# Attention readout and a top-2 expert layer: four experts' numbers to a register word

## Chip, cores and metric

The kernel runs on one core of a Trainium2 chip. The metric is the time of one execution on the device in microseconds, lower is better. A measurement is several runs of the same program, and its median stands for it.

## What is computed

`x` is 64 x 128 rows of 512 numbers in float32. Two steps follow each other, each added to its input:

```python
x = x + _L0_xattn_ref(_layernorm(x), ctx_2048, mask)     # 64 batches of 128 rows, 128 context rows each
x = x + _L0_ffn_ref(_layernorm(x), G, gate_w, up_w, down_w, lora_A, lora_B)

# the second step, with 8 experts of width 64, top 2, and a low-rank part of 16
scores = softmax(einsum('bsh,he->bse', x, G))
value, indices = top_k(scores, 2)
w = einsum('bsk,bske->bse', value, one_hot(indices, 8))
gated = silu(einsum('bsh,efh->bsef', x, gate_w)) * einsum('bsh,efh->bsef', x, up_w)
out = einsum('bsef,bse,ehf->bsh', gated, w, down_w)
lr  = einsum('bsh,erh->bser', x, lora_A)
out = out + einsum('bser,bse,ehr->bsh', lr, w, lora_B)
```

## The kernel before

**The sweep** (`for t in range(SWEEP)` on each engine, up to about 220 us) goes over the 64 batches of 128 tokens: layer norm, attention, the new x, and the router's logits. It picks each token's two experts and scatters the token's row (x, weights, row numbers) to a table in HBM, `x1_rows`, sorted by expert. The first expert of a token (the lower number) belongs to the first pass, the second to the second pass.

**The block loop** (`for t in range(TICKS)`) then works on blocks of 128 rows of one expert each: NQ = 70 blocks in a pass, 140 in all, and 143 ticks. SyncE loads block q's rows into one of RI = 21 slots (`load_block`), TensorE, ScalarE and VectorE work on it over four ticks, and GpSimd scatters the result: in the first pass 516 KB of rows to `z_rows`, in the second 256 KB to the output. In tick t TensorE does, in this order: `turn_h(t)`, four transposes (L478); `gate_up(t-1)`, four float32 matmuls of 144 columns that the hardware does in eight pieces (L494), whose weights lie at an address that depends on the block's expert; the register load `expert_at(t+1)` (L487); `turn_gated(t-2)`, one transpose (L501); `down(t-3)`, two matmuls of 512 columns (L510, L511), again at the expert's address. ScalarE copies the transposed rows (L658), does the tanh (L664), the rounded half of the gated values (L670) and, in the first pass, the layer norm (L651). VectorE makes `t` (L1061), `gg` (L1066), the other half `ggT_b` (L1073) and two copies (L1077, L1078), and adds the block's result to its rows (L1088), with one more instruction, L1087, where a block may overlap the next. `down` waits for L1078 of the tick before (semaphore `again`), L501 for L1066 of the tick before (`gg_ready`).

Which expert a block belongs to is known only once the tokens have been counted. VectorE works out a table with a column for each of the two passes: the expert times WE = 576 (the width of an expert's weights) and the first row. It stands with blocks along the partitions. `turn_table` on TensorE turns it by four matmuls against the identity, and `keep_table` on VectorE copies partition 64 of the result to `table_i`, where registers are loaded from. This happens twice: for the first KA = 38 blocks of each pass during the sweep (t = 54), and for the other 32 in tick 27 of the block loop; VectorE's arithmetic for the second table is spread over ticks 8 to 23. TensorE loads a block's expert by `pe.value_load` (L487), SyncE its first row (L286): each a register load, one fused register instruction and an assertion that the value is in range. Nothing schedules the work: the order of each engine is the order written here.

## Time and profile before

| what | us |
|---|---|
| median of 3 runs (545.64 to 547.66) | 546.95 |
| the profiled execution, device time | 547.48 |
| its span from first to last instruction | 545.7 |
| TensorE matmuls busy | 513.9 |
| VectorE busy | 477.7 |
| ScalarE busy | 357.8 |
| GpSimd busy | 287.0 |

All times inside an execution are read against its span, which is 1.8 us shorter than its device time. The sweep ends at about 220 us. The first pass of the block loop takes TensorE from there to about 390 us and the second pass to about 540. "PEld" is the row of TensorE's weight loads, of which each matmul has one, and a q behind an engine (PEldq, SPq) its sequencer, which executes register loads, register arithmetic and waits itself.

### The profile page before, as it was taken

Reading aid. Unit: us, or ns where it says so; the run is one execution under the profiler, and the core shown is the slowest. Engines: PE = TensorE matmul, PEld = TensorE weight load, DVE = VectorE, ACT = ScalarE, POOL = GpSimd, SP = SyncE. Lnnn points to the kernel's source line nnn. Section 1 sums busy time; section 2 is a strip of 40 time slices with the busy share of each in tenths; the row PEclk is TensorE's granted clock in tenths of the full one; section 3 lists DMA queues with packets and bytes.
Section 4 is the critical chain, followed back from the end, with each engine's and each line's share of the span. In section 5 each row is a group of like instructions: output and inputs, shape, how many; then the busy total and the mean of one; then the engine's idle time right before and its main releaser. Section 6 shows DMA issues by size and latency. Waiting matters only on the chain.

```text
span 545.7 us, 16991 instructions
## 1 busy us (share of the span) xinstructions
PE 513.9 (94%) x4040; PEld 441.5 (81%) x4040; DVE 477.7 (88%) x1919; ACT 357.8 (66%) x991; POOL 287.0 (53%) x398
## 2 busy tenths in 40 slices
PE   8999999999999999698999899999999999999994
PEld 7788877778877877587788788888899999999883
DVE  5899999999999997668898888888899999999875
ACT  4778888888887876566677677777544444444441
POOL 4237677776776665644444344344444445444434
PEclk9999999999999999999999999999999999999988
DMA  8999999999999979999997999857999999999722
GB/s 312 355 323 360 387 389 361 401 386 393 388 392 384 320 246 299 397 376 400 360 328 278 365 364 330 301 215 261 411 413 416 416 415 417 415 416 412 290 97 77
DMA packets 65611, 189.13 MB, mean 347 GB/s; under 512 B 9582, under 2 KB 9710, under 8 KB 65520
## 3 DMA queue, kind: packets, MB, share of 16 engines
q1 hardware_dynamic: 44352, 120.20, 59.9%
q0 software_dynamic: 20800, 67.65, 31.6%
q8 instruction: 40, 0.66, 0.5%
q14 instruction: 51, 0.42, 0.2%
q10 hardware_dynamic: 368, 0.21, 0.1%
HBM read 114.03 MB, written 78.73 MB: 353 GB/s over the span
## 4 chain that ended last, share of the span: by engine, by line
PE 80%; issue 7%; DVE 5%; ACT 4%; another core or an unknown queue 1%; POOL 1%; DMA 0%; POOLq 0%; DVEq 0%; ACTq 0%
PE rd L494 12%; PE bank L494 12%; PE bank L478 11%; PE bank L348 8%; PE rd L510 8%; PE rd L511 6%; PE rd L393 6%; PE rd L394 4%; PE rd L501 4%; PE bank L329 4%; PE bank L361 3%; ACT xn L588 1%; PE bank L385 1%; ACT pT L559 1%; PE bank L346 1%
## 5 line engine op out<-in xcount | busy, mean ns | idle before, releaser
L658 ACT COPY hT<-bank 128x512 f32<-128x512 f32 x140 | 82.0, 586 | 61.8 <-PE bank L478 51.5
L494 PE MATMUL bank<-wg_sb,hT 128*128 x560 | 80.5, 287 | 1.9 <-ACT hT L658 1.8
L494 PE MATMUL rd<-wg_sb,hT 128*128 x560 | 82.2, 291 | 0.1
L1193 POOL DMA_INDIRECT x_rows<-xe x64 | 65.3, 1020 | 29.7 <-issue 21.4
L494 PEld LDWEIGHTS rd<-wg_sb,hT 128*128 128x128 f32 x560 | 74.4, 194 | 0.4 <-issue 0.3
L494 PEld LDWEIGHTS bank<-wg_sb,hT 128*128 128x128 f32 x560 | 72.6, 190 | 2.6 <-issue 2.6
L348 PE MATMUL bank<-cc_sb,xnT 128*128 128x136 f32 x512 | 73.0, 285 | 0.0
L510 PE MATMUL rd<-dn_a,ggT_a 128*128 x140 | 67.6, 483 | 1.6 <-DVE ggT_b L1078 1.2
L348 PEld LDWEIGHTS bank<-cc_sb,xnT 128*128 128x128 f32 x512 | 63.7, 190 | 2.1
L1208 POOL DMA_INDIRECT out_x<-z_shared x41 | 40.1, 977 | 43.4 <-issue 26.8
L1088 DVE SCALAR_TENSOR_TENSOR z_shared<-rd,z_shared 128x512 f32<-128x512 f32 x77 | 57.7, 749 | 1.9 <-PE rd L511 0.2
L1205 POOL DMA_INDIRECT z_rows<-z_own x34 | 32.9, 967 | 50.1 <-DVE z_own L1088 41.5
L1205 POOL DMA_INDIRECT z_rows<-z_shared x36 | 34.7, 965 | 46.5 <-DVE z_shared L1088 38.2
L511 PE MATMUL rd<-dn_b,ggT_b 128*128 x140 | 55.9, 399 | 0.0
L588 ACT ACTIVATE xn<-x_sb,norm 128x512 f32<-128x512 f32 x64 | 51.7, 808 | 1.1 <-POOL std L1145 1.1
L1088 DVE SCALAR_TENSOR_TENSOR z_own<-rd,z_own 128x512 f32<-128x512 f32 x63 | 47.2, 749 | 1.5
L501 PE MATMUL rd<-const_sb,gg 128*96 128x128 f32 x140 | 39.1, 279 | 9.8 <-issue 6.4
L751 DVE SCALAR_TENSOR_TENSOR xe<-rd,rinv,x_sb 128x512 f32<-128x512 f32 x64 | 47.7, 745 | 0.6 <-issue 0.6
L693 DVE BATCH_NORM_STATS2 st<-x_sb 128x6 f32<-128x512 f32 x64 | 43.7, 682 | 4.6 <-DMA x_sb<-in_x 4.3
L478 PEld LDWEIGHTS bank<-const_sb,z_shared 128*128 128x128 f32 x308 | 38.7, 142 | 10.7 <-issue 0.2
L478 PE MATMUL bank<-const_sb,z_shared 128*128 128x128 f32 x308 | 46.4, 273 | 0.0
L393 PE MATMUL rd<-cc_sb,pT 128*128 128x256 f32 x128 | 43.8, 424 | 1.2 <-ACT pT L559 0.6
(168 smaller groups left out, 1202.1 us busy)
## 6 DMA issues: line engine op xcount, KB each, us to landing
cc_sb<-in_cc SPq DMA_DIRECT2D x64, 532.0 KB
z_shared<-z_rows SPq DMA_DIRECT2D x41, 516.0 KB
x_sb<-in_x SPq DMA_DIRECT2D x64, 256.0 KB
z_own<-z_rows SPq DMA_DIRECT2D x29, 516.0 KB
z_shared<-x_rows SPq DMA_DIRECT2D x36, 260.0 KB
z_own<-x_rows SPq DMA_DIRECT2D x34, 260.0 KB
z_rows<-pad SPq DMA_DIRECT2D x8, 516.0 KB
wg_sb<-in_wg SPq DMA_DIRECT2D x8, 288.0 KB
```

The costliest lines, as they stand in the source:

```text
L348: mm = pe.matmul(sc_ps[:, 0:S + E], xnT[:, n % 2, k, :], by_feature(n, k, S + E), start=False, stop=(k == KD - 1))
L393: pe.matmul(rd_ps[n % 2][:, RD:512], pT[:, n % 2, :], cc_sb[:, n % RC, 0:512 - RD], start=True, stop=True)
L478: mm = pe.transpose(hT_ps[q % 2][:, k * P:(k + 1) * P], rows_of(q)[:, k * P:(k + 1) * P], ident)
L494: mm = pe.matmul(gu_ps[q % 2][:, 0:GU], hT[:, q % 2, k, :], wg_flat[:, bass.ds(at + k * GU, GU)], start=(k == 0), stop=(k == KD - 1))
L501: pe.transpose(gT_ps[0:KG, 0:P], gg[:, q % 2, :], ident).then_inc(ggT_done, 1)
L510: pe.matmul(y_ps[j][:], ggT_a[:, j, :], a_flat[:, bass.ds(at, D)], start=True, stop=False)
L511: pe.matmul(y_ps[j][:], ggT_b[:, j, :], b_flat[:, bass.ds(at, D)], start=False, stop=True).then_inc(y_done, 1)
L588: act.activation(xn[:, n % 2, :], x_sb[:, n % RX, :], ACT.Identity, scale=norm[:, m % 2, 0, b, 1:2], bias=norm[:, m % 2, 0, b, 0:1]).then_ ...
L658: act.copy(hT[:, q % 2, :, :], hT_ps[q % 2][:].rearrange("p (k s) -> p k s", k=KD)).then_inc(hT_ready, 1)
L1088: dve.scalar_tensor_tensor(out=row[:, D:2 * D], in0=y_ps[q % 2][:], scalar=row[:, weight:weight + 1], in1=row[:, D:2 * D], op0=ALU.mult, o ...
L1193: pool.indirect_dma_start(out=x1_rows[:, :], out_offset=rows_at(row, ROW1), in_=row, in_offset=None, bounds_check=ROWS - 1, oob_is_err=Fal ...
L1205: pool.indirect_dma_start(out=z_rows[:, :], out_offset=rows_at(row, D + ROW2), in_=row, in_offset=None, bounds_check=ROWS - 1, oob_is_err= ...
```

## The change

The word that TensorE loads no longer holds one expert times 576 but the experts of up to four consecutive blocks, three bits each. A pass has 38 and 32 blocks in its two tables, thus 10 and 8 groups, and both passes 36 groups. `turn_table` makes the words: for the two expert columns it multiplies by a constant matrix, `PACK`, that holds 1, 8, 64 and 512 for a group's four blocks, where the identity stood. VectorE's `keep_table` copies words and first rows apart, to `packed` and `first_row`. `expert_at` loads a word at the first block of a group (blocks 0, 4, 8 ... 36, 38, 42 ... 66 of a pass), keeps it in a register, and takes the expert out by a division, a remainder and a multiplication by 576. The constants grow by 18 columns. SyncE's loads of first rows are as they were, from the other tile.

```diff
@@ -59,6 +59,11 @@
+GB, EB = 4, 3
+assert E <= 1 << EB
+GROUPS = [range(at, min(at + GB, hi)) for lo, hi in ((0, KA), (KA, NQ)) for at in range(lo, hi, GB)]
+EARLY_GROUPS = -(-KA // GB)
...
@@ -137,7 +142,8 @@
-        expert, table, table_i = sb("expert", [2]), sb("table", [4]), sb("table_i", [4, NQ], I32)
+        expert, table, first_row = sb("expert", [2]), sb("table", [4]), sb("first_row", [2, NQ], I32)
+        packed = sb("packed", [2, len(GROUPS)], I32)
...
-                first = sp.value_load(table_i[KEPT:KEPT + 1, 2 + k, at:at + 1], min_val=0, max_val=ROWS - P)
+                first = sp.value_load(first_row[KEPT:KEPT + 1, k, at:at + 1], min_val=0, max_val=ROWS - P)
...
-            def turn_table(i, lo, hi):
+            def turn_table(i):
+                (lo, hi), (first, last) = blocks_of(i), groups_of(i)
                 pe.wait_ge(table_ready, 2 * i + 2)
                 for k in range(4):
-                    at = TABLES[i] + k * (hi - lo)
-                    mm = pe.matmul(rt_ps[:, at:at + hi - lo], table[:, k:k + 1].broadcast_to([P, P]), ident[:, lo:hi], start=False, stop=True, skip_group_check=True)
+                    what = const_sb[:, PACK + first:PACK + last] if k < 2 else ident[:, lo:hi]
+                    at = TABLES[i] + (k * (last - first) if k < 2 else 2 * (last - first) + (k - 2) * (hi - lo))
+                    mm = pe.matmul(rt_ps[:, at:at + what.shape[1]], table[:, k:k + 1].broadcast_to([P, P]), what, start=False, stop=True, skip_group_check=True)
                 mm.then_inc(tabT_done, 1)
...
+            word = {}
             def expert_at(q):
                 k, at = divmod(q, NQ)
+                g = next(i for i, group in enumerate(GROUPS) if at in group)
                 if q == 0:
                     pe.wait_ge(tabT_ready, 1)
                 if q == KA:
                     pe.wait_ge(tabT_ready, 2)
-                return pe.value_load(table_i[KEPT:KEPT + 1, k, at:at + 1], min_val=0, max_val=(E - 1) * WE)
+                if at == GROUPS[g].start:
+                    word[0] = pe.value_load(packed[KEPT:KEPT + 1, k, g:g + 1], min_val=0, max_val=(1 << EB * GB) - 1)
+                return pe.snap(word[0] // (1 << EB * (at - GROUPS[g].start)) % (1 << EB) * WE, min_val=0, max_val=(E - 1) * WE)
...
-                dve.tensor_scalar(table[:, 0:2], expert[:], float(WE), None, ALU.mult).then_inc(table_ready, 1)
+                dve.tensor_scalar(table[:, 0:2], expert[:], 1.0, None, ALU.mult).then_inc(table_ready, 1)
...
-            def keep_table(i, lo, hi):
+            def keep_table(i):
+                (lo, hi), (first, last) = blocks_of(i), groups_of(i)
+                at = TABLES[i] + 2 * (last - first)
                 dve.wait_ge(tabT_done, i + 1)
-                dve.tensor_copy(table_i[KEPT:KEPT + 1, :, lo:hi],
-                                rt_ps[KEPT:KEPT + 1, TABLES[i]:TABLES[i] + 4 * (hi - lo)].rearrange("p (k q) -> p k q", k=4)).then_inc(tabT_ready, 1)
+                dve.tensor_copy(packed[KEPT:KEPT + 1, :, first:last], rt_ps[KEPT:KEPT + 1, TABLES[i]:at].rearrange("p (k g) -> p k g", k=2))
+                dve.tensor_copy(first_row[KEPT:KEPT + 1, :, lo:hi],
+                                rt_ps[KEPT:KEPT + 1, at:at + 2 * (hi - lo)].rearrange("p (k q) -> p k q", k=2)).then_inc(tabT_ready, 1)
...
+    for i, group in enumerate(GROUPS):
+        consts[list(group), PACK + i] = 2.0 ** (EB * np.arange(len(group)))
```

TensorE's queue in tick 27, from the last pieces of `gate_up` over the register load, `turn_gated`, `down` and the second table to the next tick. Before:

```order
L494 ISA
L494 MATMUL bank2<-wg_sb,hT 128x144
L487 TENSOR_LOAD table_i
L487 ISA x2
L501 MATMUL rd0<-const_sb,gg 96x128
L510 REGISTER_ALU
L510 MATMUL rd1<-dn_a,ggT_a 128x512
L511 REGISTER_ALU
L511 MATMUL rd1<-dn_b,ggT_b 128x512
L434 MATMUL bank3<-const_sb,table 128x32 x4
L478 MATMUL bank0<-const_sb,z_own 128x128 x4
```

The same place in the change, block 28 beginning a word, where L515 is `gate_up`, L507 the load, L522 `turn_gated`, L531 and L532 `down`, L449 `turn_table` and L493 `turn_h`:

```order
L515 ISA
L515 MATMUL bank2<-wg_sb,hT 128x144
L507 TENSOR_LOAD packed
L507 ISA x2
L522 MATMUL rd0<-const_sb,gg 96x128
L531 REGISTER_ALU
L531 MATMUL rd1<-dn_a,ggT_a 128x512
L532 REGISTER_ALU
L532 MATMUL rd1<-dn_b,ggT_b 128x512
L449 MATMUL bank3<-const_sb,table 128x8 x2
L449 MATMUL bank3<-const_sb,table 128x32 x2
L493 MATMUL bank0<-const_sb,z_own 128x128 x4
```

And in the tick after it in the change, where block 29 takes its expert out of the word that is there:

```order
L515 ISA
L515 MATMUL rd0<-wg_sb,hT 128x144
L522 MATMUL rd0<-const_sb,gg 96x128
L531 REGISTER_ALU
L531 MATMUL rd1<-dn_a,ggT_a 128x512
L532 REGISTER_ALU
L532 MATMUL rd1<-dn_b,ggT_b 128x512
L493 MATMUL bank1<-const_sb,z_shared 128x128 x4
```

The load and its two ISA rows (the fused instruction and the assertion) are gone between `gate_up` and `turn_gated` in three ticks of four, and no row has come for taking the expert out: these operations are part of the ISA row ahead of a block's first matmul of `gate_up`. That row holds two register operations before, and four or five in the change.

VectorE's queue in the sweep where the first table is copied, before and then in the change (L815 is L794, L756 is L735):

```order
L794 MAX_INDEX which<-top,lg 128x8
L964 CAST table_i<-bank 1x4x38
L735 ISA masked,rowmin<-bank,zeros 128x128
L735 ISA rowmin 128x1
L742 RECIPROCAL rinv<-rowsum 128x1
```

```order
L815 MAX_INDEX which<-top,lg 128x8
L987 CAST packed<-bank 1x2x10
L988 CAST first_row<-bank 1x2x38
L756 ISA masked,rowmin<-bank,zeros 128x128
L756 ISA rowmin 128x1
```

One copy of 152 elements has become one of 20 and one of 76; in the block loop one of 128 becomes one of 16 and one of 64.

## Rows read from the trace of the kernel before

**Rows 1.** The page, part 1: engine, busy us (share of the span), instructions.

```profile
PE 513.9 (94%) x4040; PEld 441.5 (81%) x4040; DVE 477.7 (88%) x1919; ACT 357.8 (66%) x991; POOL 287.0 (53%) x398
```

**Rows 2.** By stretch: PE, PEld, DVE, ACT, POOL busy; clock, DMA share, GB/s.

```profile
235.00:312.00 77.00, 71.69 (x485) 60.64 (x483) 65.67 (x231) 52.84 (x127) 33.77 (x35) 1.00 0.95 350
312.00:401.00 89.00, 86.88 (x592) 75.06 (x591) 76.37 (x256) 62.56 (x150) 37.57 (x39) 1.00 0.88 321
401.00:509.00 108.00, 108.00 (x808) 100.07 (x807) 101.29 (x341) 51.50 (x162) 52.10 (x55) 1.00 1.03 415
...
150.00:187.00 37.00, 35.53 (x317) 29.43 (x316) 35.90 (x186) 29.71 (x87) 25.44 (x40) 1.00 1.01 375
```

**Rows 3.** Line L501 in 235:312, 312:401 and 401:509, with two idle rows (both TensorE rows together).

```profile
L501 PEld LDWEIGHTS rd<-const_sb,gg x31: 123/124/127, 236.0 to 310.4; 128*96 128x96 f32 x31
...
  issue: 11.9, 26
...
L501 PEld LDWEIGHTS rd<-const_sb,gg x40: 123/124/128, 312.7 to 400.9; 128*96 128x96 f32 x40
...
  issue: 6.2, 18
...
L501 PEld LDWEIGHTS rd<-const_sb,gg x54: 124/127/129, 400.9 to 507.4; 128*96 128x96 f32 x54
```

**Rows 4.** TensorE's weight loads by line, 235:312 and 312:401: busy, mean ns | idle before, releasers.

```profile
L510 PEld LDWEIGHTS rd<-dn_a,ggT_a 128*128 128x128 f32 x31 | 5.8, 187 | 3.1 <-issue 1.2
L501 PEld LDWEIGHTS rd<-const_sb,gg 128*96 128x96 f32 x31 | 3.9, 124 | 8.1 <-issue 7.6 <-DVE gg L1066 0.4
...
L510 PEld LDWEIGHTS rd<-dn_a,ggT_a 128*128 128x128 f32 x39 | 7.3, 187 | 3.4 <-issue 0.6
L501 PEld LDWEIGHTS rd<-const_sb,gg 128*96 128x96 f32 x40 | 5.0, 125 | 5.4 <-issue 4.6
```

**Rows 5.** Line L487 in the same stretches: ns min/median/max, first and last start.

```profile
L487 PEldq TENSOR_LOAD <-table_i x31: 297/766/1424, 236.9 to 311.7; - x31
...
L487 PEldq TENSOR_LOAD <-table_i x40: 298/616/1257, 311.7 to 400.0; - x40
L487 PEldq FUSED_REGOPS  x40: 151/151/151, 312.2 to 400.4; - x40
...
L487 PEldq TENSOR_LOAD <-table_i x54: 296/328/523, 401.9 to 508.3; - x54
```

**Rows 6.** Weight loads in order of time, 338.9 to 341.9, and its first register load.

```profile
339.02 1.04 PEld L494 LDWEIGHTS rd<-wg_sb,hT 128*128 128x128 f32 x8
340.31 0.12 PEld L501 LDWEIGHTS rd<-const_sb,gg 128*96 128x96 f32 x1 [0.24 <-issue]
340.52 0.19 PEld L510 LDWEIGHTS rd<-dn_a,ggT_a 128*128 128x128 f32 x1
...
341.42 0.67 PEld L494 LDWEIGHTS bank<-wg_sb,hT 128*128 128x128 f32 x5
...
L487 PEldq TENSOR_LOAD <-table_i x1: 842/842/842, 339.0 to 339.0; - x1
```

**Rows 7.** VectorE: largest waits in 235:401, and one copy of the tick of rows 6.

```profile
DVE t L1061 <- ACT th L664: 11.5, 31, 1.7
DVE t L1061 <- issue: 1.4, 2, 1.1
...
339.54 0.22 DVE L1078 CAST ggT_b<-ggT_a 32x128 fp32r<-32x128 f32 x1
```

**Rows 8.** Added work's nearest rows: L494's register operations (340.9:341.3), L964, L931, the constants.

```profile
L494 PEldq FUSED_REGOPS  x3: 42/46/46, 341.0 to 341.2; - x3
...
L964 DVE CAST table_i<-bank x2: 290/301/312, 187.7 to 292.7; 1x152 int32<-1x152 f32 x1, 1x128 int32<-1x128 f32 x1
...
L931 DVE TENSOR_SCALAR table<-expert x2: 163/181/199, 184.2 to 284.1; 128x2 f32<-128x2 f32 x2
...
const_sb<-in_consts ACTq DMA_DIRECT2D x1, 179.5 KB, 3.3
```

More of the change, by code:

```diff
@@ L81 @@
 RI = RO + RS
-IDENT, BEFORE, BASE, ROW0, LAST0, IOTA, NEXT, PART, SIGN, LOW, IDS, STRIPS = np.cumsum(
-    [0, P, P, 2 * E, 2 * E, 2 * E, E, SEG, 1, 1, 1, TB]).tolist()
-NCONST = STRIPS + 2 * E
+IDENT, BEFORE, BASE, ROW0, LAST0, IOTA, NEXT, PART, SIGN, LOW, IDS, STRIPS, PACK = np.cumsum(
+    [0, P, P, 2 * E, 2 * E, 2 * E, E, SEG, 1, 1, 1, TB, 2 * E]).tolist()
+NCONST = PACK + len(GROUPS)
 def xattn_moe(nc, x, cc, mask, wg, dn, g, consts, out):
@@ L231, in in_sweep, with blocks_of, groups_of @@
             return 0 <= t - stage < B
+        def blocks_of(i):
+            return ((0, KA), (KA, NQ))[i]
+        def groups_of(i):
+            return ((0, EARLY_GROUPS), (EARLY_GROUPS, len(GROUPS)))[i]
         def in_tick(t, stage):
@@ L467, in _ @@
                     pe.wait_ge(place_ready, BA + 1)
-                    turn_table(0, 0, KA)
+                    turn_table(0)
             def turn_h(q):
@@ L540, in _ @@
                 if t == TABLE:
-                    turn_table(1, KA, NQ)
+                    turn_table(1)
                 if t == SKIP:
@@ L1041, in _ @@
                 if t == EARLY_TABLE:
-                    keep_table(0, 0, KA)
+                    keep_table(0)
             stats_x1(B - 1)
@@ L1121, in _ @@
                 if t == TABLE:
-                    keep_table(1, KA, NQ)
+                    keep_table(1)
                 if t == SKIP - 2 * PACE:
```

## The prediction

> **What bounds the kernel now.** I read the page's busy line first [rows 1]: TensorE is busy for 94% of 545.7 us, VectorE for 88%, the others for 66% and less. So TensorE leads, with VectorE close behind it, and the question is where TensorE is not full. The table of stretches [rows 2] says it. From 401 to 509 us its matmul row is busy for 108.00 of 108 us, in 235 to 312 for 71.69 of 77, in 312 to 401 for 86.88 of 89. A matmul's end is modelled, so these shares flatter it. The pace tells more: L501 runs once a tick, and its first and last starts [rows 3] give 76.7 us for the 31 ticks from 236.0 to 312.7, that is 2.474 us each; 88.2 us for the 39 up to 400.9, 2.262 each; and 106.5 us for the 53 up to 507.4, 2.009 each. In the last the matmul row has no hole, so 2.009 us is what the array itself needs for a tick. Against it the first 31 ticks lose 76.7 - 31 x 2.009 = 14.4 us and the next 39 lose 88.2 - 39 x 2.009 = 9.8 us: **24.2 us in all, nearly all of them in the first pass**.
>
> Who takes them? In the idle column of the weight loads [rows 4] the array waits 8.1 and 5.4 us before L501 and 3.1 and 3.4 us before L510. That is 20.0 us, and somewhat more in truth, since a weight load's modelled end lies 0.07 us behind the point at which the next could start (eight in 1.04 us with 190 ns each are 0.12 apart), which over the 44 waits of L501 (26 and 18 of them) [rows 3] adds 3 us. The sum meets the 24.2. The releaser is "issue": no other engine. Ahead of L501 in TensorE's own queue stands L487, the register load of the expert of the next tick's block, and its duration is the key [rows 5]: median 328 ns, 523 at most, from 401 on, but median 766 and up to 1424 ns in 235 to 312 and 616 and up to 1257 ns in 312 to 401. One tick shows how it bites [rows 6]: the load starts at 339.0, takes 842 ns, 151 ns of fused register operations [rows 5] and an assertion follow, and L501 can start at 340.31, some 0.4 us after the load's end, where the last of L494's eight weight loads had left room at about 340.0. A load begins about 1.0 us ahead of L501's turn, with eight weight loads queued, so what passes roughly 0.6 us of it is exposed. After 401 none is.
>
> The Trainium skill (Perfetto Trace Analysis, Sequencer Loop) describes it so: engine instructions are pushed into a queue, control instructions are executed by the sequencer itself. By another page (DMA: Bandwidth & Descriptors, Latency and other measured facts) such a load has a floor of about 600 ns; if every load here took that, all would just be covered and the change would give next to nothing. The trace does not agree at either end: 296 ns at the least, and a median above 600 in the whole first pass.
>
> **What the change takes away.** 104 of 140 loads go, each with its fused instruction and assertion. In the second pass that is worth nothing: L494's queued work covers the load there, and the 2.009 us stay. In the first pass, a load for block t+1 stands in tick t, and remains when block t+1 begins a word. Of the 31 ticks 8 keep theirs (blocks 8, 12 ... 36), of the 39 ticks 10 (38, 42 ... 74, over the pass's end). So 23/31 of 14.4 and 29/39 of 9.8 us could go: 10.7 + 7.3 = **18.0 us, the upper end**.
>
> **What VectorE gives back.** I do not count on all of it. VectorE has in 235 to 312 65.67 us of work and in 312 to 401 76.37 [rows 2]. To it comes about 0.11 us per tick of gaps between its instructions, in which nobody is waited for (from 401 to 509 VectorE is short of the stretch by 6.7 us in 54 ticks, 0.12 each). It thus needs 65.7 + 3.4 = 69.1 us and 76.4 + 4.4 = 80.8 us. Its idle time before L1061 in these stretches is 11.5 + 1.4 = 12.9 us [rows 7], with little elsewhere: hardly more than that can go while its work stays. TensorE would need 66.0 and 80.9 us (31 x 2.009 + 3.7, 39 x 2.009 + 2.5, with the exposures that stay). If the two needs fell together perfectly, the larger of them would count, 69.1 and 80.9, a gain of 7.6 + 7.3 = 14.9 us. If a kept exposure and VectorE's surplus never overlapped, they would add: in the first stretch 69.1 + 3.7 = 72.8, a gain of 3.9 us; in the second VectorE has no surplus over 39 x 2.009 = 78.4 but 2.4 us, so 80.8 + 2.5 = 83.3, a gain of 4.9 us. That is 8.8 us. The place where VectorE holds TensorE is L510, which waits for L1078 of the tick before; in the tick of [rows 6, 7] L1078 ends at 339.76 and L510 starts at 340.52, of which the stall gave 0.24 us, so in an unstalled tick only a few tenths are spare. In the first stretch VectorE also makes the second table, some 0.2 us an instruction (as L931 of [rows 8]), five or so in every third tick, and runs late just there. Little spare argues for the additive end. I take **10.5 us**.
>
> **What it adds, term by term.** (1) Taking the expert out of the word: the order shows no new instruction; the first ISA row of L494 now holds four or five register operations for two. L494's fused instructions of two and three (multiply, add) take 42 to 46 ns [rows 8], L487's of two comparisons and a logical one 151 ns [rows 5]. Division and remainder are not in the trace; two to three more operations at 4 to 50 ns each are 0.01 to 0.15 us, and I take 0.1. They stand where the array has the tail of L478 before it: in the tick of [rows 6, 8] L494's first fused operation starts at 341.0 and its first weight load at 341.42, some 0.35 us of cover, so I cost them at nothing, except that a kept load starts later by as much: 18 x 0.1, at most 1.8 us, of which I count 0.5. (2) VectorE's keep_table makes two copies instead of one of 290 and 312 ns [rows 8]. The big one gets shorter (76 and 64 elements for 152 and 128), the small one is like L931's 163 ns. Nothing to +0.2 us each; in the sweep VectorE is busy for 35.90 of 37 us around it [rows 2], so the first is on the path, the second about so: +0.3 us. (3) turn_table's first two matmuls have 10 and 8 columns for 38 and 32: at most 0.1 us less, counted at nothing. (4) 18 more columns of constants on 359, on a transfer of 3.3 us at the start [rows 8]: 0 to +0.15, taken as 0.1. Together +0.9 us. SyncE's own 140 loads stay, and its ring runs a dozen blocks ahead.
>
> **Sum.** 10.5 - 0.9 = 9.6 us less. The profiled execution took 547.48 us (span 545.7), so 537.9; that run lies 0.5 us above the median of 546.95, so against the median **537.4 us**.
>
> **Rivals.** *No give-back*: VectorE follows and all 18.0 us go, minus 0.9, 529.8 us. For it: nowhere in 312 to 401 does VectorE have table work. Against it: L510's wait, and that VectorE has only 12.9 us of waits to give. *The kept loads grow*: a shorter first pass moves the same bytes in less time; the long loads come with the first pass's scatters, and 350 GB/s in 235 to 312 [rows 2] would be 375 or so. If the 18 kept loads expose half as much again (+3.1 us) and VectorE takes the additive end (8.8), the gain is 8.8 - 3.1 - 0.9 = 4.8 us: 542.1 us. The transfer engines' share is 0.95 and 0.88 already [rows 2]. *Nothing to see*: the wait before L501 is not the load but the trip behind it or another engine's lateness, which takes its place at once (gg of L1066 is named once with 0.4 us [rows 4]): 546 us. *Slower, by the extraction*: if divide and remainder cost x us in the sequencer, every tick pays once x passes the 0.35 us of cover, 137 ticks x (x - 0.35). From x = 0.42 on that eats the gain; at x = 0.6 it costs 34 us against 10 gained, 571 us, and at 0.45 it is 14 against 10: about 551 us. For it: no row shows a division, and a comparison, (151 - 34) / 3 = 39 ns by [rows 5], already costs ten times the 4 ns of a multiply or add. Against it: each of the two or three operations would have to cost four times a comparison.
>
> **How the numbers follow.** Forecast 0.60 (533 to 540.5, from gains of 14.9 and 8.8 minus costs), no give-back 0.11, kept loads grow 0.15, nothing to see 0.07, slower 0.07. The range reaches from 532 to 544: it leaves out most of the no give-back case below it and the last two cases above it. A measurement of this kernel can tell some 0.5%, 2.7 us, from no change. Faster by more than that has 0.60 + 0.11 + 0.15 = 0.86, same 0.07, slower 0.07.
>
> **What would show it.** TENSOR_LOAD 36 times, 18 of them in the first pass with the old durations. Idle before L501 down from 8.1 + 5.4 to some 4 us, in kept ticks alone. A second pass unchanged at 2.0 us a tick. Idle before L510 left or grown, now with VectorE's L1078 as its releaser, and VectorE's waits for th down from 12.9 us to a few. The first fused operation of a tick at 0.05 to 0.2 us. I am wrong if the second pass slows (extraction), if ticks without a load still wait before L501, or if VectorE keeps its idle time.

## The result and the profile after

The changed kernel takes **539.7 us** (median of four executions, 537.3 to 541.3) against 547.25 (545.64 to 547.66) for the kernel before beside it: a ratio of 0.986 with a 95% interval of 0.983 to 0.989. In a second comparison, described below, it was 0.983 (0.979 to 0.986). The forecast was 537.4, range 532 to 544. The profiled execution of after is the quickest of its four: 537.3 us, span 535.5, that is 10.2 us below the profiled execution of before (547.5).

The page of after, part 1, as in [rows 1]: as many matmuls as before, but 11.0 us less of busy time (their ends are modelled, so no work has gone), and 2.9 us less on VectorE with two instructions more.

```profile
PE 502.9 (94%) x4040; PEld 436.6 (82%) x4040; DVE 474.8 (89%) x1921; ACT 353.1 (66%) x991; POOL 286.8 (54%) x398
```

The stretches of after, with the columns of [rows 2]; they hold the same 31, 39 and 53 ticks as those of before (L522 is now what L501 was, L531 is L510, L507 is L487, L515 is L494, L1085 is L1061, L1102 is L1078).

```profile
235.00:311.00 76.00, 69.30 (x482) 59.87 (x482) 65.24 (x229) 51.50 (x124) 33.76 (x35) 1.00 0.97 359
311.00:391.50 80.50, 79.66 (x587) 72.90 (x587) 72.86 (x255) 58.59 (x149) 37.66 (x39) 1.00 0.91 338
391.50:499.00 107.50, 107.00 (x798) 98.63 (x797) 99.94 (x336) 50.91 (x159) 51.45 (x53) 1.00 1.03 415
```

From the start of the same block's L501 or L522 to that of another (blocks 3, 34, 73, 126, as in [rows 3]) the time went like this, in us:

| stretch | before | after | difference | predicted |
|---|---|---|---|---|
| 31 ticks from 236 | 76.6 | 75.7 | -0.9 | -3.9 to -7.6 |
| 39 ticks | 88.3 | 80.6 | -7.7 | -4.9 to -7.3 |
| 53 ticks, second pass | 106.5 | 107.5 | +1.0 | 0 |
| all ahead of and behind them | | | -2.6 | +0.4 (additions) |

So the sum of 10.2 comes close to the 9.6 that was forecast for the profiled execution, but its parts do not, and that they add up is partly luck: the first stretch gave almost nothing, and 2.6 us came from outside the three stretches, 1.1 ahead of them and 1.5 behind. Two profiles of the kernel before differ by 2.1 us in the part behind (38.3 and 36.2), so that part can't be put down to the change. Here are the idle columns of after's weight loads in 235:311 and 311:391.5 (they answer to [rows 4]), and L507's loads up to 401 and behind it (to [rows 5]).

```profile
L531 PEld LDWEIGHTS rd<-dn_a,ggT_a 128*128 128x128 f32 x32 | 6.0, 188 | 5.9 <-issue 5.3
...
L522 PEld LDWEIGHTS rd<-const_sb,gg 128*96 128x96 f32 x32 | 4.0, 125 | 4.9 <-issue 3.2 <-DVE gg L1090 1.4
...
L531 PEld LDWEIGHTS rd<-dn_a,ggT_a 128*128 128x128 f32 x40 | 7.6, 189 | 1.2 <-issue 0.7
L522 PEld LDWEIGHTS rd<-const_sb,gg 128*96 128x96 f32 x39 | 4.9, 126 | 1.1 <-issue 1.0
```

```profile
L507 PEldq TENSOR_LOAD <-packed x20: 296/720/1255, 229.5 to 395.1; - x20
...
L507 PEldq TENSOR_LOAD <-packed x15: 297/318/530, 403.2 to 514.4; - x15
```

L522's wait fell from 8.1 to 4.9 and from 5.4 to 1.1 us; L531's doubled in the first stretch, 3.1 to 5.9, and went from 3.4 to 1.2 in the second. The releaser that is printed is "issue", but one tick without a load tells whose wait it is. Both fences are of after; first VectorE in order of time, then the weight loads.

```profile
293.75 0.75 DVE L1112 SCALAR_TENSOR_TENSOR z_own<-rd,z_own 128x512 f32<-128x512 f32 x1
294.42 0.25 DVE L959 TENSOR_TENSOR bounds<-const_sb,filled 128x16 f32<-128x16 f32 x2
294.70 0.21 DVE L961 TENSOR_TENSOR jump<-bounds 128x48 f32<-128x48 f32 x1
294.95 0.21 DVE L963 TENSOR_TENSOR jump<-jump,past 128x48 f32<-128x48 f32 x1
295.19 0.20 DVE L965 TENSOR_REDUCE over<-jump 128x2 f32<-128x48 f32 x1
...
296.33 0.22 DVE L1102 CAST ggT_b<-ggT_a 32x128 fp32r<-32x128 f32 x1
```

```profile
296.12 0.12 PEld L522 LDWEIGHTS rd<-const_sb,gg 128*96 128x96 f32 x1
296.71 0.19 PEld L531 LDWEIGHTS rd<-dn_a,ggT_a 128*128 128x128 f32 x1 [0.46 <-issue]
```

Five instructions of table work push VectorE's next tick back by 0.9 us; L1102 ends at 296.55 and L531, which waits for it, starts at 296.71, 0.46 us late. In the kernel before, the exposure of a register load often stood ahead of such a wait and could cover part of it. How much of the first stretch's shortfall is VectorE's is asked further below, where a second cause shows up. VectorE itself had less to wait for than in [rows 7]; the two stretches of after:

```profile
DVE t L1085 <- ACT th L685: 5.5, 5, 2.5
...
DVE t L1085 <- ACT th L685: 2.3, 6, 0.5
```

### The profile page after: what moved, and what is told of

The parts are those of the page before. It is cut to its first block, busy times and chain, and to the rows that moved or that the text cites. A ratio compares the mean times of both kernels' runs of the same rounds, so it can differ in the third digit from the quotient of the medians.

```text
span 535.5 us, 16681 instructions
## 1 busy us (share of the span) xinstructions
PE 502.9 (94%) x4040; PEld 436.6 (82%) x4040; DVE 474.8 (89%) x1921; ACT 353.1 (66%) x991; POOL 286.8 (54%) x398
## 4 chain that ended last, share of the span: by engine, by line
PE 70%; issue 8%; DVE 7%; DMA 6%; ACT 4%; SPq 3%; another core or an unknown queue 1%; POOL 1%; POOLq 0%; DVEq 0%; ACTq 0%
PE bank L515 10%; PE rd L515 10%; PE bank L493 9%; PE bank L361 8%; PE rd L531 6%; PE rd L406 6%; PE rd L532 5%; PE rd L407 4%; PE bank L342 4%; PE bank L374 3%; PE rd L522 3%; DMA z_shared<-z_rows 3%; DMA x_sb<-in_x 2%; ACT xn L609 1%; SPq L299 1%
## 5 line engine op out<-in xcount | busy, mean ns | idle before, releaser
L515 PE MATMUL bank<-wg_sb,hT 128*128 x560 | 80.5, 287 | 2.0 <-ACT hT L679 1.2
L515 PE MATMUL rd<-wg_sb,hT 128*128 x560 | 80.2, 286 | 0.0
L515 PEld LDWEIGHTS bank<-wg_sb,hT 128*128 128x128 f32 x560 | 72.6, 190 | 2.7 <-issue 2.7
L515 PEld LDWEIGHTS rd<-wg_sb,hT 128*128 128x128 f32 x560 | 72.6, 190 | 0.1
L531 PE MATMUL rd<-dn_a,ggT_a 128*128 x140 | 66.9, 478 | 5.1 <-issue 2.6
L1232 POOL DMA_INDIRECT out_x<-z_shared x41 | 39.9, 973 | 43.7 <-issue 31.8
L532 PE MATMUL rd<-dn_b,ggT_b 128*128 x140 | 55.2, 395 | 0.0
L493 PEld LDWEIGHTS bank<-const_sb,z_shared 128*128 128x128 f32 x308 | 38.2, 140 | 11.0 <-DMA z_shared<-z_rows 0.8
L493 PE MATMUL bank<-const_sb,z_shared 128*128 128x128 f32 x308 | 46.2, 272 | 0.2 <-DMA z_shared<-z_rows 0.2
L522 PE MATMUL rd<-const_sb,gg 128*96 128x128 f32 x140 | 38.5, 275 | 7.4 <-DVE ggT_b L1097 3.2
```

Of the source, the lines that this page charges most:

```text
L493: mm = pe.transpose(hT_ps[q % 2][:, k * P:(k + 1) * P], rows_of(q)[:, k * P:(k + 1) * P], ident)
L515: mm = pe.matmul(gu_ps[q % 2][:, 0:GU], hT[:, q % 2, k, :], wg_flat[:, bass.ds(at + k * GU, GU)], start=(k == 0), stop=(k == KD - 1))
L522: pe.transpose(gT_ps[0:KG, 0:P], gg[:, q % 2, :], ident).then_inc(ggT_done, 1)
L531: pe.matmul(y_ps[j][:], ggT_a[:, j, :], a_flat[:, bass.ds(at, D)], start=True, stop=False)
L532: pe.matmul(y_ps[j][:], ggT_b[:, j, :], b_flat[:, bass.ds(at, D)], start=False, stop=True).then_inc(y_done, 1)
```

## The experiments

The executions of one comparison share the kernel before, and only ratios are set side by side across comparisons: in the first (word2, word8, one_load) it took 546.9 us, in the second (keep_140, dummies, the two spreadings) 533.5, in the third (after_again and the three with it) 545.9, in the last 533.6. Words of one block, meant as the control with all loads kept, have no time: their wider table did not fit into SBUF, and keep_140 takes its place.

**How many loads matter.** Words of two and of eight blocks, and one single load for the whole kernel (every block then takes its expert from the first word, so other experts than the table's are used and the output is wrong; all other instructions and all sizes are the same).

```diff
-GB, EB = 4, 3
+GB, EB = 2, 3        (word2)
+GB, EB = 8, 3        (word8)
...
-                if at == GROUPS[g].start:
+                if q == 0:        (one_load)
```

> Words of two blocks: 70 loads, 35 in the first pass. If the gain goes with the loads removed, two thirds of the change's 7.5 us (70 of 104 loads): 542 us. If it is worth less per load at first, because a neighbour's load covers for it or VectorE gives the time back, 544 to 545.

> Words of eight blocks, 24 bits each: 18 loads, 9 in the first pass instead of 18. Nine more loads of about 0.35 us exposed each: 2 to 3 us less than the change, 537 us. If VectorE now holds the first pass, 0.5 us less or nothing: 539.5.

> One load in all: the word of blocks 0 to 3 serves every block, so the experts of the others are wrong ones, while all addresses, sizes and instructions stay as they are. It is the floor for what loads cost. My theory (VectorE and the second table's arithmetic hold the rest of the first pass): 18 loads of the change give another 4 to 5 us, 535 us, with 235 to 311 us still at 2.3 us a tick or more in ticks without a load. Rival (without loads the array runs at its own pace): both stretches at 2.01 us a tick, 530 us or less.

Measured: word2 538.2 us, 0.983 (0.978 to 0.988); word8 534.8 us, 0.977 (0.972 to 0.981); one_load 531.2 us, 0.971 (0.966 to 0.976). The 31 and 39 ticks took 74.0 and 81.6 us, 73.6 and 79.6, 71.4 and 79.1. Word2 and word8 came out quicker than either of their expectations, one_load between its two. Word2 with 70 loads is thus hardly worse than after with 36 (the intervals overlap), because a load that is short enough is free: of its 35 loads in the two stretches half expose nothing, and the exposures ahead of L522 sum to 5.2 us, as after's do (5.1). In word8 they are 2.1. The weight loads of one_load in 235:311, which has no load at all:

```profile
L531 PEld LDWEIGHTS rd<-dn_a,ggT_a 128*128 128x128 f32 x33 | 6.2, 189 | 5.0 <-issue 5.0
L522 PEld LDWEIGHTS rd<-const_sb,gg 128*96 128x96 f32 x33 | 4.1, 125 | 2.5 <-issue 2.4
```

7.5 us of waits are left without one load, and the 31 ticks still take 71.4 us where 31 x 2.009 would be 62.3; the second stretch has no such remainder, 79.1 against 78.4. So of the loss that the prediction counted, the loads account for 5.2 of 14.4 us in the first stretch (76.6 to 71.4) and for 9.2 of 9.8 in the second (88.3 to 79.1). VectorE's table work stands in the first stretch alone and is the obvious holder of the rest, but this run does not show that it is the only one; *What the stands hide*, below, comes to another.

**The change without its aim.** All 140 loads stay, the rest is the change.

```diff
-                if at == GROUPS[g].start:
+                if True:
```

> All 140 register loads stay, one ahead of each block, each reading the four-block word again; the expert is taken out of the word in registers exactly as in the changed kernel, and VectorE's two copies, the two short matmuls and the constants are the changed kernel's too. So everything is in it but the 104 loads that went. Theory (the loads' exposure is the whole gain, the extraction is free but for its 0.1 us ahead of an exposed load): back to the kernel before or just over it, 547 to 550 us (547 + 0.9 for the additions of my sum + up to 44 exposures x 0.05 us). Rival (the gain came from something else that the change brought, such as the shorter table work or another instruction order): it stays near 540.

Measured: 541.3 us, 1.013 (1.006 to 1.019) times before. Both theories of the expectation are off: the gain does hang on the loads, but the additions, with all loads kept, cost 7.8 us (541.3 - 533.5) and not 1 to 3. The second pass, where next to nothing had been exposed, tells of 4.3 of them. In order: the stretches of keep_140 (31, 39 and 53 ticks), and its loads in the last.

```profile
234.00:306.70 72.70, 70.22 (x481) 59.99 (x481) 64.69 (x229) 53.30 (x124) 33.78 (x35) 1.00 1.02 389
306.70:396.00 89.30, 86.25 (x585) 74.50 (x585) 76.02 (x255) 62.28 (x149) 37.74 (x39) 1.00 0.86 316
396.00:507.00 111.00, 111.00 (x799) 100.00 (x799) 100.64 (x336) 51.51 (x159) 51.63 (x53) 1.00 1.02 409
```

```profile
L507 PEldq TENSOR_LOAD <-packed x53: 302/373/668, 397.1 to 506.0; - x53
```

The 53 ticks take 110.8 us, 2.09 each, for 106.5. The loads are somewhat longer than before's (median 373 for 328), but the main thing is the length from which one is exposed. For each tick with a load, this is how much later than the regular 122 ns L501 or L522 starts behind the start of the last weight load of L494 or L515 (137 ticks of each kernel, some lengths shown):

| load of ... ns | before: ticks, median delay | keep_140 |
|---|---|---|
| 400 to 449 | 6, 1 ns | 11, 4 ns |
| 450 to 499 | 5, 0 | 15, 24 |
| 500 to 549 | 14, 2 | 11, 115 |
| 550 to 599 | 5, 59 | 10, 160 |
| 600 to 649 | 6, 127 | 9, 182 |
| 650 to 699 | 5, 201 | 4, 259 |
| 700 to 749 | 5, 236 | 3, 298 |

Exposure begins at a load shorter by somewhat under 0.1 us, and for a load of the same length the delay is some 55 to 115 ns larger. That is about the price of the division and the remainder, 73 ns a tick (below): they stand ahead of L515's weight loads and the load behind them, so their time is taken from the run-ahead. After mostly escapes this cost because three of four ticks have no load. The Trainium skill (Perfetto Trace Analysis, Sequencer Loop), cited in the prediction, has one sequencer read an engine's instructions in turn, push the engine's own into a queue and execute control instructions itself; the shift in this table agrees with that.

**A longer extraction.** Fourteen register operations for the division and the remainder.

```diff
-                return pe.snap(word[0] // (1 << EB * (at - GROUPS[g].start)) % (1 << EB) * WE, ...)
+                e = word[0] // (1 << EB * (at - GROUPS[g].start)) % (1 << EB)
+                for m in (5, 7, 11):
+                    e = (e * m + 1) // m % (1 << EB)
+                return pe.snap(e * WE, ...)
```

> The changed kernel with a longer way of taking the expert out of the word: after the division and the remainder three more rounds of multiply, add, divide, remainder that leave the value as it is (with other factors each), so 14 operations for 2 ahead of L515's first weight load in every tick. The extraction's 0.10 to 0.15 us should become x = 0.4 to 0.6 us. The step of the prediction: cover 0.35 us, so every tick pays x - 0.35, at x = 0.5 137 x 0.15 = 20 us more, and nothing below x = 0.35. Rival (the operations have no cover at all, or none where VectorE is the one that waits): 137 x 0.35 = 48 us more, or, if the sequencer runs further ahead than I read, nothing.

Measured: 546.4 us, 1.004 (1.001 to 1.007), that is 11.2 us above the changed kernel in the same comparison. The operations were cheaper than I had assumed: what stands ahead of L518's weight loads is 402 ns a tick (median), for 253 in after and 180 in before, so x is 0.22 us and below the 0.35 of cover, and by the prediction's step nothing should show. Against after_again the three stretches grew by 3.3, 4.2 and 2.8 us (some of the 3.3 is ScalarE's, see below). In the second pass 13 of the 14 ticks with a load in the stretch pay 0.06 to 0.33 us before L525 (L522 in after) although their loads are short, and the tick right behind a load some 0.09 us more; the ticks after that stand at 2.00 us for the most part. One tick with a load, in order of time, and the load in it, which in the kernel before would have exposed nothing:

```profile
416.75 0.93 PEld L518 LDWEIGHTS bank<-wg_sb,hT 128*128 128x128 f32 x7
417.91 0.12 PEld L525 LDWEIGHTS rd<-const_sb,gg 128*96 128x96 f32 x1 [0.23 <-issue]
```

```profile
L507 PEldq TENSOR_LOAD <-packed x1: 437/437/437, 417.0 to 417.0; - x1
```

So ticks two or more behind a load cover the 0.22 us, as the prediction's cover of 0.35 us has it (a cover as long as 0.35 was not tried); the kept loads and the tick behind each have none to spare.

**Has VectorE room in the first stretch?** Thirty more VectorE instructions that nobody reads, five in each of the ticks 9, 12 ... 24.

```diff
+                if t in range(9, 25, 3):
+                    for i in range(5):
+                        dve.tensor_scalar(spare[:, range(9, 25, 3).index(t) * 5 + i, :], const_sb[:, 0:2], 1.0, None, ALU.mult)
                 if t == TABLE:
                     keep_table(1)
```

> The changed kernel with 30 more small VectorE instructions whose result nobody reads, five behind the work of each of the ticks 9, 12 ... 24, that is between the ticks in which the second table is made. They are like L952's row, about 160 ns each with 0.02 us to the next: 5 us of VectorE work. Theory (VectorE and its table arithmetic set the pace of the first 31 ticks, since the run with one single load still took 71.4 us for them): nearly all of it shows, 4 to 5 us, 543.5 to 545 us. Rival (VectorE waits 5.5 us for th there, so it has room, and the stretch is held by the transfers, whose share is 0.97): 1.5 us or less, 541 us at most.

Measured: 523.8 us, 0.981 (0.977 to 0.985), no slower than the changed kernel's 0.986 and 0.983. The changed kernel itself was not run in this comparison, so the cost is bounded only roughly; in the trace the dummies' ticks show a delay of 0.24 us before L532 in five of six cases, 1.2 us in all. But the dummies were not the 5 us of work that the expectation counted. None of them waits for another, and they overlap; one group and its neighbours on VectorE:

```profile
242.86 0.75 DVE L1113 SCALAR_TENSOR_TENSOR z_own<-rd,z_own 128x512 f32<-128x512 f32 x1
243.52 0.44 DVE L1148 TENSOR_SCALAR spare<-const_sb 128x2 f32<-128x2 f32 x5
243.87 0.22 DVE L1086 SCALAR_TENSOR_TENSOR t<-th,rd 128x64 f32<-128x64 f32 x1
```

They start 0.07 us apart, and five of them hold back L1086 by 0.35 us, where four instructions of the table, each waiting for the one before, stand 0.2 us apart and take 0.7. The six groups thus took 2.1 us of VectorE's time, of which 1.2 shows as delay. So this run does not show that VectorE has room; at most some 0.9 us of theirs found place. The groups of the table themselves stand in the same trace: of L532's 4.4 us of waits there some 3 are behind them, up to 0.6 us at a time. The next kernels take the groups apart.

**The groups taken apart.** The same 26 and 9 instructions, one or two a tick instead of three to six in every third.

```diff
-                if t == SHARED + PACE:
-                    late_counts()
-                ... (five more groups, every third tick)
+                if SHARED + PACE <= t < TABLE:
+                    take(late, 2 if t < SHARED + PACE + 7 else 1)
...
+                if SKIP - 2 * PACE <= t < SKIP:
+                    take(last, 2)
```

> The changed kernel with the 26 VectorE instructions of the second table taken apart: not in six groups of three to six in every third tick, but two a tick in ticks 8 to 14 and one a tick in 15 to 26; the nine of the overlap two a tick from 28 on. Same instructions, same order among themselves. Theory (a group makes VectorE late by a whole microsecond at once, the array stands, and in the next tick VectorE stands for th in turn, so the lateness of one is not paid back by the other): the 2 to 3 us of VectorE's waits for th in 235 to 311 go, 537 us. Rival (only the sum of VectorE's work counts, or the loads hold those ticks anyway): no change, 539.7 us.

> The same spreading on the kernel with words of eight blocks (18 loads, 534.8 us, 73.6 us for the first 31 ticks). With five loads left in the first stretch the groups of table work are nearly all that holds it. VectorE's need there is about 69.5 us (66 of work and 0.11 us of gaps a tick). Theory (groups cost more than their sum): 70.5 to 71.5 us for the 31 ticks and 532 to 532.5 us in all. Rival (only the sum counts): 534.8 us.

Measured: 519.75 us, 0.974 (0.970 to 0.978), and 518.85 us, 0.973 (0.969 to 0.977). The 31 ticks took 66.0 us in both (dummies, in the same comparison: 69.7), well below the 70.5 to 71.5 that was expected of spread_word8. L532's wait, which was 5.9 us in after, in spread_word4, 231.3:297.2:

```profile
PEld rd L532 <- issue: 1.6, 7, 0.3
```

The distance to the dummies' kernel is 3.7 us in the 31 ticks, for dummies that took 2.1 us. This looked like a clean win over after, and it speaks for groups costing more than their sum, by 1.6 us or more, though after itself was not in this comparison. The third comparison tested it with all three kernels side by side.

> The changed kernel once more, beside the kernel before with a profile of each. Chips differ: on the one of the first comparison the kernel before took 547 us, on the one of the dummies and the spreading 533.5. If this chip is like the second: the ratio to before stays at 0.986 plus or minus 0.004 by one theory (what the loads cost is the same everywhere), or falls to 0.975 by the other (on the second chip TensorE's start of the first pass has no stalls of 2 us, so VectorE has less to hide and more of the removed exposure comes through; the kernel with 30 dummies had 0.981 there and spread_word4 0.974).

> The kernel before itself, for its profile on this chip: ratio 1.000. Expected of the profile if the chip is the faster one: a first pass of 85 to 88 us for the 39 ticks of the later stretch as before, and 69 to 72 us for the first 31 ticks, because keep_140, which has the same loads, took 72.4 there.

> The kernel with the second table's VectorE instructions taken apart, now beside the changed kernel on one chip. Theory (groups of five at once cost more than their sum): 3 to 5 us below the changed kernel, 66 us for the first 31 ticks against 69.7 or more. Rival (only the sum of VectorE's work counts): equal to the changed kernel within 1 us.

Measured: after_again 535.2 us, 0.983 (0.979 to 0.986); before_again 546.6 us, 1.001 (0.998 to 1.005); spread_again 537.1 us, 0.986 (0.983 to 0.989). The 31, 39 and 53 ticks: before 76.5, 89.2, 106.5; after 72.7, 80.9, 107.4; spread 74.6, 81.6, 106.1. Here the first stretch gave 3.8 us, the additive end of the prediction, and the spreading brought nothing. In its trace ScalarE stands three times for over 2 us, ahead of L523 of blocks 10, 13 and 16, and once for 1.4 us ahead of block 7's, and all others follow. One of them, in order of time (L680 copies hT, L686 makes th, L673 normalises a row):

```profile
248.98 0.59 ACT L680 COPY hT<-bank 128x512 f32<-128x512 f32 x1 [0.78 <-PE bank L494]
252.01 0.22 ACT L686 ACTIVATE th<-bank 128x64 f32<-128x64 f32 x1 [2.44 <-PE rd L516]
```

And TensorE's weight loads then:

```profile
250.11 1.04 PEld L516 LDWEIGHTS rd<-wg_sb,hT 128*128 128x128 f32 x8
...
253.09 0.12 PEld L523 LDWEIGHTS rd<-const_sb,gg 128*96 128x96 f32 x1 [1.95 <-DVE gg L1120]
```

The same four places of ScalarE's stream (its instructions 925 to 927, 946 to 948, 967 to 969 and 988 to 990, three ticks apart) show stands of 0.8 to 3.0 us in every profile of the first and third comparison, before, after and one_load alike, and none above 0.6 us in the second and the last, where the kernel before was 13 us quicker. (A profile of before is at hand for the first and third only.) The first of the four in before, after and one_load:

```profile
243.66 0.59 ACT L658 COPY hT<-bank 128x512 f32<-128x512 f32 x1 [2.06 <-remote]
...
242.76 0.59 ACT L679 COPY hT<-bank 128x512 f32<-128x512 f32 x1 [2.06 <-PE bank L493]
...
242.94 0.59 ACT L679 COPY hT<-bank 128x512 f32<-128x512 f32 x1 [1.47 <-PE bank L493]
```

Do they explain the missing gain? The last run asks it.

> Words of eight blocks and the second table's VectorE instructions taken apart, a second time and on whichever chip comes. On the chip where ScalarE had no unexplained stands the ratio to before was 0.973 and the first 31 ticks took 66.0 us. On the next chip the spreading of the changed kernel brought nothing (0.986 against 0.983), and in its trace ScalarE stood three times for 2.4 to 3.0 us at its instructions 948, 969 and 990 with nobody to wait for. If that is what ate it, then a profile without such stands shows 66 to 67 us for the 31 ticks and a ratio of 0.973 to 0.976, and one with them shows 66 us plus their sum, 72 to 74 us, and a ratio of 0.98 or above. If instead the spreading itself costs (VectorE late in every tick), the 31 ticks take over 72 us without any stand of ScalarE.

Measured: 519.1 us (six executions) against 533.6, 0.977 (0.971 to 0.982); the two medians by themselves give 0.973, and one of before's eleven executions, at 526.6, lies far below the rest. The profile has no stand there and 66.0 us for the 31 ticks, 78.5 for the 39:

```profile
231.80:297.70 65.90, 65.78 (x479) 58.50 (x479) 61.39 (x229) 50.91 (x124) 33.71 (x36) 1.00 1.03 403
297.70:376.30 78.60, 78.56 (x588) 72.81 (x587) 73.03 (x255) 58.30 (x149) 37.50 (x40) 1.00 0.96 369
```

The forecast for a profile without stands holds in the 31 ticks, and in the ratio about. Spread_again's stretch in the same columns is the other case, with 8.6 us more and VectorE's work the same to 0.8 us:

```profile
234.70:309.30 74.60, 67.32 (x481) 59.02 (x480) 62.20 (x229) 50.71 (x125) 33.65 (x35) 1.00 0.96 358
```

**What the stands hide.** The stands lie in the 12 ticks from L501 (L522) of block 6 to that of block 18. Set apart from the other 19 ticks of the first stretch, in us:

| kernel, loads in the 31 ticks | 12 ticks | other 19 |
|---|---|---|
| with stands: before, 31 | 31.7, 30.7 | 44.9, 45.7 |
| word2, 15 | 31.7 | 42.3 |
| after, 8 | 31.7, 29.6 | 44.0, 43.1 |
| word8, 4 | 31.8 | 41.8 |
| one_load, 0 | 30.3 | 41.1 |
| long_extraction, 8 | 30.9 | 45.1 |
| spread_again, 8 | 33.1 | 41.4 |
| without stands: keep_140, 31 | 26.6 | 45.8 |
| dummies, 8 | 27.3 | 42.4 |
| spread_word4, 8; spread_word8 and spread8_again, 4 | 25.3 | 40.7 |

With stands the 12 ticks take about as long with 31 loads as with 4, and 30.3 us without any; without stands they take 26.6 us even with all 31 loads and the added operations. In before, the exposures of 0.5 to 1.0 us ahead of L501 of blocks 7, 10, 13 and 16 fall right behind the four stands, 3.1 us in all. So in these 12 ticks the loads mostly took time that was lost already, and the change had little to gain. Nor do the kernels without stands show a gain there (26.6 with 31 loads, 27.3 with 8 loads and the dummies); it shows in the other 19 ticks, 45.8 against 42.4. This also tells that one_load's 71.4 us is no floor of VectorE's: the 12 ticks are 3.0 us longer in it than in the dummies' kernel, which has 8 loads and 30 instructions more.

What the stands are is not settled. They are there in one_load, so the loads don't make them. No transfer and no other engine is named as the one waited for (once TensorE's already finished L516, else "remote"), the few instruction transfers in that time (0.3 and 1.0 us each) fall together with one of the three at most, and no run took one suspected cause away. Nor do we know what sets the two kinds of comparison apart: the record gives the first comparison, with stands, and the last, without, the same chip number. So words of eight with the groups taken apart is the best kernel of the study at 0.973 and 0.977, both against a kernel before that took 533.5 us, though spread_word4 (0.974) and word8 in the first comparison (0.977) lie within its interval; that it beats after where before takes 546 us was not shown, and for four-block words it did not.

## Why the prediction was right, and where it was not

- **The load's exposure as the loss to be had.** Right in kind: with one load left the gain was 15.7 us (546.9 to 531.2), and with all of them kept it was gone. In size it is right for the second stretch (9.2 of 9.8 us) and too large for the first (5.2 of 14.4). The idle before L501 was to fall to some 4 us, in kept ticks alone; it fell to 6.0 (4.9 and 1.1). With the 0.07 us that a modelled end hides, the delays are 7.4 us, 5.1 in ticks with a load and 2.3 in others.
- **VectorE's give-back, first stretch: the mis-sized term.** I took VectorE's floor for 31 ticks as its work and gaps, 69.1 us, and counted what the stretch lost above that as the loads'. The gain was to be 3.9 to 7.6 and was 0.9 in one profile and 3.8 in the other. The floor is wrong: the same instructions, taken apart, ran in 66.0 us where ScalarE did not stand. What was missing are two terms. One is ScalarE's stands, which are in the trace that I predicted from (2.1, 1.7, 1.2 and 1.0 us) and which I did not look for; the 12 ticks around them took 31.7 us in before and in after. The other is table work in groups, each delaying TensorE at once by up to 0.6 us. How the shortfall divides between the two was not measured, since after was not run where there are no stands. One place shows how such time goes. From L501 of block 7 to that of block 8 before took 2.48 us with 0.40 of a load's exposure in it, and after 2.59 with no load, so the exposure was worth nothing there. But the group of table work in that tick does not explain it: in the dummies' kernel, with the same group and no stand ahead, the same tick took 2.00. In after, VectorE had just waited 2.5 us for th behind ScalarE's stand, and L531 waited 0.41 for VectorE.
- **VectorE's give-back, second stretch: also mis-sized, the other way.** 4.9 to 7.3 was forecast, 7.7 and 8.4 came. The loads' exposures in these ticks fell from 7.1 to 1.5 us, so about 2 us more went than they took. The work of 76.4 us [rows 2] was not fixed: it is 72.9 in after, though the instructions are the same. L1078's and L1102's median stays at 220 ns, but the largest fell from 491 to 379 and the mean from 261 to 226. A duration that is long now and then was thus longer where TensorE stalled more, and a sum of durations is no floor.
- **The second pass is worth nothing.** Right that it gives no gain; it costs 0.9 to 1.0 us (53 ticks: 107.5 and 107.4 for 106.5). Behind the border of the passes TensorE now waits for rows to land, which no row of before showed; the sum had no such term. The weight loads' waits of after_again in its second pass:

```profile
PEld bank L493 <- DMA z_own<-z_rows: 1.0, 2, 0.6
PEld bank L493 <- DMA z_shared<-z_rows: 0.8, 1, 0.8
```

- **Additions.** The first fused operation of a tick came out at 93 to 157 ns (median 130) for 42 [rows 8], so 0.05 to 0.12 us where 0.1 was estimated. "Hidden except at kept loads" is right for this change; with the longer extraction the tick behind a kept load pays too. But the price in the rival *slower, by the extraction* was wrong: it starts at no threshold of 0.35 us, but at once, in the ticks with a load. At x = 0.22 over before, of which after has 0.07 already, it costs 11 us more than after, all of the gain.
- **A slip in the range.** The 533 to 540.5 of "how the numbers follow" does not come out of its own terms: the additive gain of 8.8 less the costs of 0.9 is 7.9, and 546.95 - 7.9 is 539.0. Neither the forecast nor the stated range of 532 to 544 rests on it.
- **Rivals.** No give-back (529.8) did not come: even one_load stayed above it. Kept loads that grow: the kept ones had a median of 835 ns in the first stretch and 596 in the second, in after_again 878 and 666, for 766 and 616 [rows 5], so a tenth or so, worth less than the 3.1 us of that rival. Nothing to see and slower fell with the first result.
- **Signs.** 36 loads and the first fused operation came as said. VectorE's waits for th were to fall from 12.9 us to a few and fell to 7.8, of which 5.5 are five waits of up to 2.5 us in the stretch of the stands. That ticks without a load still wait before L522 was named as a sign that I am wrong, and they do, for 2.3 us in all in the first stretch, 0.9 of it behind VectorE's late gg after a stand; it marks just the term that failed.

## What to carry to other kernels

A register load that an engine's own sequencer has to wait for costs only what exceeds the work queued ahead of it; so count the long ones, and know that anything put ahead of the load in the same queue, even 70 ns of register arithmetic, is taken from that cover. Before a stall is priced at its full length, look at the ticks in which another engine is late anyway, and list the waits of every engine there, not only of the two busiest: where both fall together, taking one away gives little. A kernel with the stall removed altogether measures in one run what the stall is worth; who holds the rest takes another run. A filler that is to stand for real work has to be chained like it, or it overlaps and weighs less: look at its rows before its result is read. Bursts of small dependent work on an engine with little slack are better spread, as far as these runs go.

## What the runs showed of the hardware

- A TENSOR_LOAD of one word from SBUF took from 295 to 1462 ns in these runs: 306 to 383 in the median for the blocks behind 73, where the first pass's scatters had ended, and 469 to 751 for blocks 4 to 73, by no clear rule of how many are made.
- A division and a remainder, in the fused instruction that also adds: 0.05 to 0.12 us more. Twelve more of them, partly multiplications and additions: 0.15 us more a tick, less than I had put for them.
- Five VectorE instructions on 128x2 elements that wait for nothing started 0.07 us apart, though each took 0.16 us and more; a chain of four on 128x16, each waiting for the one before, 0.2 us apart.
- The same program differs by 2.5% between comparisons (533.5 and 546 us for the kernel before), and two profiles of the same kernel (spread_word4 and spread_again, spans 518.3 and 532.8) put 8.6 us of it into the first 31 ticks, 2.8 just ahead of them and 1.7 behind the 53 ticks of the second pass, and in all three places ScalarE stands for 1.1 to 3.0 us in spread_again. A change of 1% there is only readable within one comparison.
